# Halves for the values of the second cross attention, scores two rows ahead, and the float8 weight rounded among the experts

## What is computed

```
def _L1_xattn_ref(query, key, value, Wq, bq, Wk, bk, Wv, bv, Wo, bo):
    q = query @ Wq.T + bq;  k = key @ Wk.T + bk;  v = value @ Wv.T + bv
    attn = softmax(einsum('bqh,bkh->bqk', q, k) * 64 ** -0.5, axis=1)   # over the 100 queries
    return (attn @ v) @ Wo.T + bo

def fp8_gemm_optimized(x, input_scale, kernel, kernel_scale):
    x_q = (x / input_scale[0]).astype(float8_e4m3fn)
    k_q = (kernel / kernel_scale[0]).astype(float8_e4m3fn)
    return (x_q @ k_q) * (input_scale[0] * kernel_scale[0])
```

## Time and profile before

| | us |
|---|---|
| median of 3 runs | 1007.02 (1004.06 to 1007.10) |
| profiled execution, time | 1005.17 |
| profiled execution, span | 1003.4 |
| TensorE busy | 927.7 (92%) |
| VectorE busy | 429.6 (43%) |
| ScalarE busy | 346.2 (35%) |
| GpSimd busy | 250.9 (25%) |
| mean TensorE clock granted | 0.956 |

### The profile page before, as it was taken

The page is one execution under the profiler, slowest core; times in us unless marked ns, Lnnn a source line. Parts: engine busy times, 40 slices in busy tenths (PEclk is TensorE's granted clock), DMA queues, the critical chain, the costliest instruction groups (busy, mean ns, idle before and its releaser), DMA issues. The chain is left out here.

```text
span 1003.4 us, 19157 instructions
## 1 busy us (share of the span) xinstructions
PE 927.7 (92%) x7712; PEld 747.4 (74%) x7712; DVE 429.6 (43%) x994; ACT 346.2 (35%) x886; POOL 250.9 (25%) x306
## 2 busy tenths in 40 slices
PE   5999999989998889999999999998989899999992
PEld 5977776677775634789999999996865568999531
DVE  3973454224442656002112233136267731656576
ACT  3422332245552123122232233334266612221374
POOL 5451111023554316000000000005065403000275
PEclk9999999999999979899999999997969999999996
DMA  9993000245732707149999888801050032971001
GB/s 251 382 350 111 2 2 2 101 165 189 251 127 95 286 16 245 46 168 387 355 385 328 269 282 270 273 16 43 1 157 3 2 117 82 318 247 68 1 15 50
DMA packets 72456, 162.01 MB, mean 161 GB/s; under 512 B 4132, under 2 KB 5685, under 8 KB 70321
## 3 DMA queue, kind: packets, MB, share of 16 engines
q1 hardware_dynamic: 70048, 156.54, 45.7%
q0 software_dynamic: 2320, 4.25, 1.4%
HBM read 128.81 MB, written 31.97 MB: 160 GB/s over the span
## 5 line engine op out<-in xcount | busy, mean ns | idle before, releaser
L2108 PE MATMUL ps<-ffn_h,ffn_w 128*128 128x128 f32 x1280 | 149.1, 275 | 0.0
L2108 PEld LDWEIGHTS ps<-ffn_h,ffn_w 128*128 128x128 f32 x1280 | 145.9, 192 | 0.0
L2108 PE MATMUL ps<-ffn_xh,ffn_w 128*128 128x128 f32 x640 | 74.9, 275 | 0.3 <-ACT ffn_xh L2142 0.3
L2198 DVE TENSOR_SCALAR ffn_h<-ps,tile_bias 128x128 f32<-128x128 f32 x80 | 22.5, 345 | 122.4 <-PE ps L2108 122.4
L2108 PEld LDWEIGHTS ps<-ffn_xh,ffn_w 128*128 128x128 f32 x640 | 73.1, 192 | 0.9 <-issue 0.9
L1413 POOL TENSOR_TENSOR ctx_low<-shelf,ctx_high 128x1024 fp32r<-128x1024 f32 (+2 forms) x24 | 43.0, 1824 | 65.3 <-ACT ctx_high L1366 65.3
L2156 ACT ACTIVATE ffn_y<-ffn_y 128x128 f32<-128x128 f32 x80 | 23.7, 298 | 73.9 <-DVE ffn_y L2214 73.9
L2214 DVE SCALAR_TENSOR_TENSOR ffn_y<-ps,tile_bias,ffn_gate_row 128x128 f32<-128x128 f32 x80 | 22.6, 345 | 58.0 <-PE ps L2108 57.9
L1521 PE MATMUL ps<-x_qT,ctx_ct 128*128 128x100 f32 (+1 forms) x384 | 44.8, 278 | 2.3 <-PEq L137 2.0
L1521 PEld LDWEIGHTS ps<-x_qT,ctx_ct 128*128 128x128 f32 (+1 forms) x384 | 43.3, 191 | 3.7 <-issue 3.2
L2826 POOL TENSOR_TENSOR att_e<-att_e,decay 100x400 f32<-100x400 f32 x32 | 32.7, 1033 | 45.8 <-DVE att_e L2677 45.8
(11 more groups left out here) (467 smaller groups left out, 2086.6 us busy)
## 6 DMA issues: line engine op xcount, KB each, us to landing
ffn_w<-in_L_ffn_w_dram SPq DMA_DIRECT2D x60, 1024.0 KB, 5.9
shelf<-in_ctx_dram SPq DMA_DIRECT2D x12, 1280.0 KB
expert_rows<-nothing SPq DMA_DIRECT2D x1, 14820.0 KB, 49.7
context_turned<-ctx_ct SPq DMA_DIRECT2D x8, 1444.0 KB, 7.8
ctx_ct<-context_turned SPq DMA_DIRECT2D x8, 1444.0 KB, 13.8
ctx_lent<-in_ctx_dram SPq DMA_DIRECT2D x4, 1280.0 KB
rows_own<-expert_rows SPq DMA_DIRECT2D x8, 260.0 KB, 2.9
x_wo<-in_L_xattn_Wo_dram SPq DMA_DIRECT2D x1, 2048.0 KB, 8.9
```

The source lines that it names most:

```text
L2108: mm = nc.tensor.matmul(acc(n)[:, m, :], w[:, n % SLOTS, k, m * P:(m + 1) * P], into[l][:, i % 2, k, :], start=k == 0, stop=k == C - 1, sk ...
L2198: nc.vector.tensor_scalar(h2[:, i % 2, m, :], acc(n)[:, m, :], bsel[:, m, i, 1:2], 0.0, ALU.add, ALU.max).then_inc(h2_kept, 1)
```

## The change

Four edits, in one version.

1. context_columns: values from halves. ScalarE rounds the raw context (split, four pieces: columns 2 x 512, 2 x 512, 512, 512) and the shares (high_of_p), VectorE takes the rests (low_of_raw, low_of_p), TensorE does 18 float32r products of 512 columns per row with the shares stationary, and the result, now queries by features, is copied (keep_natural), turned by four transposes (turn_out) and copied again (keep_out). raw_low overwrites the raw row.
2. TensorE's order: scores(0), scores(1), then for each b scores(b+2), turn_out(b-1), value(b).
3. The context of this layer uses the three own buffers alone, and SP asks for turned row b+1 ahead of context row b.
4. kernel_piece goes to the expert stage: the weight and its scale are loaded at the end of the list `last`, and a piece follows every second unit from unit_at[10, 0] on. Both loads and a reciprocal leave the second self attention.

```
-        RAWS = 5
+        RAWS, OWN_RAWS = 5, 3
...
+            slot = b % (RAWS, OWN_RAWS)[layer]
...
                 @block.sync
                 def _(sp):
+                    sp.wait_ge(scored, 2)
+                    load_turned(sp, 2)
                     for b in range(2, B):
-                        if b >= RAWS:
-                            sp.wait_ge(used, b - RAWS + 1)
+                        if b + 1 < B:
+                            sp.wait_ge(scored, 2 * b)
+                            load_turned(sp, b + 1)
+                        if b >= OWN_RAWS:
+                            sp.wait_ge(used, b - OWN_RAWS + 1)
                         load_context(sp, 1, b)
-                        sp.wait_ge(scored, 2 * (b - 1))
-                        load_turned(sp, b)
...
-                    def value(b, c):
...
+                    def value(b):
+                        pe.wait_ge(low_p, b + 1)
+                        if b >= 1:
+                            pe.wait_ge(natural_a, b)
                         for j in range(KT):
+                            pe.wait_ge(low_raw, len(PIECES) * b + (j // 2 + 1 if j < KT - 1 else len(PIECES)))
+                            r = slice(0, keys(j))
+                            products = times(pp[r, b % 2, j, :], Pair(raw_high[b % 2], raw_low[b % OWN_RAWS])[r, j, :])
+                            for n, (p_, c_) in enumerate(products):
+                                mm = nc.tensor.matmul(ps[0:T, VB, :], p_, c_, start=j == 0 and n == 0,
+                                                      stop=j == KT - 1 and n == 2)
+                        mm.then_inc(used, 1)
...
+                    def turn_out(b):
+                        pe.wait_ge(natural_a, b + 1)
+                        if b >= 2:
+                            pe.wait_ge(out_kept, b - 1)
+                        for c in range(C):
+                            mm = nc.tensor.transpose(flip_bank(b)[:, c, :], an[:, b % 2, c * P:(c + 1) * P], ident[0:T, 0:T])
+                        mm.then_inc(flipped, 1)
 
                     scores(0)
+                    scores(1)
                     for b in range(B):
-                        if b + 1 < B:
-                            scores(b + 1)
-                        for c in range(C):
-                            value(b, c)
+                        if b + 2 < B:
+                            scores(b + 2)
+                        if b:
+                            turn_out(b - 1)
+                        value(b)
+                    turn_out(B - 1)
...
+                    split(0, range(4))
                     expo(0)
+                    high_of_p(0)
+                    expo(1)
                     for b in range(B):
+                        if b:
+                            keep_natural(b - 1)
                         if b + 1 < B:
-                            expo(b + 1)
-                        keep_a(b)
+                            high_of_p(b + 1)
+                            split(b + 1, range(4))
+                        if b:
+                            keep_out(b - 1)
+                        if b + 2 < B:
+                            expo(b + 2)
+                    keep_natural(B - 1)
+                    keep_out(B - 1)
...
+                    low_of_raw(0, (0, 1))
                     shift(0)
+                    low_of_raw(0, (2, 3))
                     share(0)
+                    shift(1)
+                    low_of_p(0)
                     for b in range(B):
+                        if b:
+                            count(b - 1)
                         if b + 1 < B:
-                            shift(b + 1)
                             share(b + 1)
-                        beside(dve, b)
-                        count(b)
+                            low_of_p(b + 1)
+                            low_of_raw(b + 1, range(4))
+                        if b + 2 < B:
+                            shift(b + 2)
+                    count(B - 1)
...
+        PIECE_AT = {unit_at[10, 0] + 2 * b: b for b in range(B)}
...
+                        (kernel_rows, natural(g["L1_ffn_kernel"]), in_kernel),
+                        (sc_k[:, 0:1], g["L1_ffn_kernel_scale"].partition_broadcast(P), in_kernel)]
...
+                    if n in PIECE_AT:
+                        b = PIECE_AT[n]
+                        if b == 0:
+                            dve.wait_ge(in_kernel, 32)
+                            nc.vector.reciprocal(sc_k[:, 1:2], sc_k[:, 0:1]).then_inc(k_step, 1)
+                        kernel_piece(dve, b)
...
-            sp.dma_start(kq[:].rearrange("p (c d) -> p c d", c=C), natural(g["L1_ffn_kernel"])).then_inc(in_f8[0], 16)
...
-            sp.dma_start(sc_k[:, 0:1], g["L1_ffn_kernel_scale"].partition_broadcast(P)).then_inc(in_f8[0], 16)
...
-                        nc.vector.reciprocal(sc_k[:, 1:2], sc_k[:, 0:1]).then_inc(ones, 1)
```

123 lines of the change are left out of this document (74 added, 49 removed).

## The result

The kernel after takes 1009.89 us (median of 11 runs, 1007.39 to 1011.51), the kernel before, run beside it, 1006.29 us (11 runs, 1002.33 to 1007.36): ratio 1.0033, 95% interval 1.0021 to 1.0046, so 2.1 to 4.6 us slower. The profiled execution of after took 1007.39 us, its span is 1005.6 us.

The account below looks back on a forecast made before the run. The prediction took a ring over VectorE and ScalarE, 11.0 us a row, as the bound. The next stage 3.2 us later, or 4.2 with low clock, put on a mean of 1005.8, gave 1010.0 us; range 1005 to 1015.

Parts of the forecast that it names:

- the stretch: Second cross attention, from the start of scores 1 to the next stage's first instruction; 85.0 us in the kernel before.
- The ring: Second cross attention: shares, high of shares, first high piece, low pieces, shift, exponentials follow one another each row, 11.0 us.
- my low bound: The ring's shortest row, 10.7 us, with low pieces and the shares' high half at their low bounds.
- TensorE's row: TensorE's work per row of the second cross attention: scores, values, transposes, row sums, 10.2 us against 11.15 before.
- Rival 1: TensorE remains the bound in the second cross attention, but faster: next stage 6.3 us earlier, 999.5 us; chance 0.07.
- The beginning: Start of the second cross attention: scores 2 wanted at 856.3, its turned row landing in time at 856.1.
- Rival 3: The turned row for scores 2 comes late, TensorE idles 6 us and low clock follows: 1014 us; chance 0.12.
- The wait at the end: TensorE idles 4.2 us ahead of row 5's transposes, whose copy stands behind expo(7) in ScalarE's queue.
- Half clock: After the idle at the end, values 6 ends 1.6 to 1.8 us later, of which about 0.9 shows.
- The weight: Moving the float8 weight's pieces from the second cross attention to the experts costs 0 us.
- rival 4: Low pieces slowed to 4.0 us by SBUF traffic, engine changes 0.08 each: ring 11.6, 1014 us; chance 0.08.

Follow-up runs that it names:

- Both cuts of the ring: The kernel after with VectorE's shift ahead of the low pieces (1006.11 us), and the kernel after with low pieces of rows 1 to 7 on GpSimd (1005.82 us).
- e4: The kernel before with only the float8 weight's move to the expert stage: 1006.06 us, ratio 1.0004 to before.
- e9: The kernel after with the float8 weight's pieces made beside the rows of the second cross attention, none among the experts: 1014.64 us, ratio 1.0101 to before.
- e1: The kernel after with VectorE's shift of row b+2 ahead of the low pieces of row b+1: 1006.11 us, ratio 1.0005 to before.
- e2: The kernel after with the low pieces of rows 1 to 7 made by GpSimd instead of VectorE: 1005.82 us, ratio 0.9999 to before.
- e3: The kernel after with ScalarE's copy of values 5 ahead of the exponentials of row 7: 1008.28 us, ratio 1.0036 to before.
- e12: The kernel after with scores one row ahead, as in before, and ScalarE's and VectorE's orders to match: 1013.12 us, ratio 1.0053 to before.
- e8: e7 with shift of row 1 ahead of row 0's shares, and values 6 in the scores' bank ahead of row 5's transposes: 1013.16 us, ratio 1.0079 to before.
- e7: e1 with ScalarE's exponentials of row b+2 ahead of the split of row b+1: 1013.76 us, ratio 1.0082 to before.
- e5: The kernel after with SP's turned row behind the wait for a free context buffer, as in before: 1088.07 us in a single run.
- e11: e1 with shift of row 1 ahead of row 0's shares and several steps of the last rows reordered: 1006.79 us, ratio 0.9998 to before.
- e10: e8 with a fourth context buffer and each context row asked for a row earlier: 1013.39 us, ratio 1.0085 to before.
- e13: e11 with context row 7 asked for right behind row 6, and row 7's high of shares between its split's halves: 1002.58 us, ratio 0.9969 to before.

## Why the prediction was right

Forecast 1010.0 us, slower by 4.2; measured 1009.89, slower by 3.3 (2.1 to 4.6). The mechanism was the one forecast. That the two times agree to 0.1 us is luck: the forecast starts from 1005.8 for before, whose median here is 1006.29, and its loss of 4.2 is too large by about as much against the 3.6 between the medians. Step by step, the stretch forecast was 939.6 - 850.44 = 89.2, measured 88.8:

- **The ring: right, 0.3 too long.** Forecast 11.0, measured 10.67, from hand-over to hand-over: shares 1.85 (forecast 1.86), high of shares 0.61 (0.74), first high piece 1.08 (1.04), low pieces 3.48 (3.63), shift 1.89 (2.0), exponentials 1.76 (1.72). I had added a change of engine where neighbours on one engine overlap. It is under my low bound of 10.7 by a hair. Both cuts of the ring gave 10.33: shown.
- **TensorE's row: 10.33, not 10.2.** Values 4.34 and not 4.2, 0.29 from the transposes to the values. This hit nothing in after, but it is what a cut of the ring can win: 0.8 a row, not 0.95. Rival 1 would have been 7 x 0.13 worse than priced.
- **The beginning: 0.7 too early.** I let scores 2 start at 5.9 us behind scores 1; it took 6.56, 1.17 of it a wait for a shift that stands behind the shares of row 0 on VectorE, an order that I had not added up. The turned row was no part of it: the first landing was 6.0 us as taken, and no scores waited for a transfer. Rival 3 is out. (Its idle was misread besides: with scores 1 done at about 855.6 and scores 2 at 863.9 it would have been 8.3 us and not 6.) The landings of ctx_ct after, as in the earlier trace rows:

```profile
DMA to landing us min/median/max: 6.0/11.8/13.3
```

- **The wait at the end: place and cause right,** 3.52 against 4.2, smaller as the ring is.
- **Half clock: undersized.** I counted 0.9 of 1.7 us as showing. Values 6 ended at about 930.0, where full speed would have given 922.70 + 0.36 + 4.34 = 927.4, so 2.6 us more; ScalarE was free at 928.1 and the copy started at 930.19, so 2.1 us showed. Six turns of the ring at 0.32 less (1.9) made up for this (1.2 more than counted) and for the beginning (0.7): the errors cancel, which is luck again, and the 0.4 by which the stretch is shorter than forecast is spread over the copies and transposes of the end.
- **The weight: 0,** shown by e4. But its value lies in the pair (e9), which I hadn't priced: I wrote that it doesn't help the second stage, meaning the kernel before.
- **Low pieces slowed (rival 4):** 1.22 and 0.68 us, as in the earlier trace rows. Out.

The rule cited in the prediction (the Trainium skill, "TensorE: Matmul & The Clock Gate", section "What's actually happening": the throttled state is the default, activity lifts it) agrees with the trace of after: 0.50 granted behind the 3.52 us of idle. It doesn't tell which idle brings the low clock; see the last section.

Over all kernels the stretch accounts for the time: against before -0.6, 0.0, 3.2, 3.8, 7.1, 8.2, 9.2, 10.0 and 81.6 us of stretch (e1, e2, e3, after, e12, e8, e7, e9, e5) go with 0.5, -0.1, 3.6, 3.3, 5.3, 7.9, 8.2, 10.2 and 81.8 us of time (the ratio's excess times 1006; for e5 the difference of the times), within about 2 us. So do 0.0, 0.2, 8.0 and -2.9 us of stretch (e4, e11, e10, e13) with 0.4, -0.2, 8.6 and -3.1.

## What to carry to other kernels

When three engines pass a tile around, write down each engine's order and add up every closed ring, not the busy time of each engine: here 10.67 us a row came from engines busy 18.8 and 13.4 of 25 us. Do it again for each reordering, since a second swap can join two rings that ran beside each other (e7). When a stage gets shorter, look next at the transfers' landing and at the last rows, where nothing lies beside the chain; and price a pair of edits as a pair. When a number comes out as forecast, look whether the event that was to bring it did happen: in e13 the row asked for earlier didn't land earlier.

## What the runs showed of the hardware that was not expected

**Two transfer engines bring up the rear.** In e11_tail_in_order context row 7 was asked for at 910.80 and landed at 925.29. Windows (last two columns: DMA share, GB/s):

```profile
914.00:916.00 2.00, 2.00 (x21) 2.00 (x21) 1.23 (x3) 0.70 (x1) 0.00 (x0) 1.00 1.06 305
...
918.00:920.00 2.00, 2.00 (x10) 1.41 (x9) 0.44 (x1) 1.53 (x2) 0.00 (x0) 1.00 0.13 49
920.00:922.00 2.00, 2.00 (x19) 1.23 (x18) 2.00 (x3) 2.00 (x5) 0.00 (x0) 1.00 0.13 47
```

By 918 the stream had thinned out; from there a share of 0.13, two of 16 engines, moved 49 and 47 GB/s up to 922, and less up to the landing. The context row's last piece is 82 partitions (L792). The Trainium skill, "DMA: Bandwidth & Descriptors", section "Why a DMA increments its semaphore by 16 and not by 1", says that a copy is spread over the largest number of engines up to 16 that divides the slowest dimension of both sides; for 82 that is 2, and the trace agrees. An estimate from the sizes in the profile's list of DMA issues and the share of two engines: per row those two carry 2/16 of 1444 and of 1280 KB and all of 164 KB, 504 KB, which at 49 GB/s is 10.5 us. The splits of e1_shift_ahead that waited for context rows came 11.3 and 11.1 us apart. Context row 7 has no turned row ahead of it: 2/16 of 1280 KB and 164 KB are 324 KB, 6.8 us by the same estimate, and its split started 6.82 us behind that of row 6 in e11 and 6.75 in e13, although it was asked for 10.3 us behind row 6 in the one and 2.8 in the other. So the row's rate of transfer seems to be set by the 82-partition piece; this is argued from two matches and was not tried. Cutting it into 80 and 2 partitions would be the next thing to measure.

**GpSimd slows VectorE's two-tensor instructions.** In e2 the share product took 1.23 us on average instead of 0.78 and the low shares, which read two tensors too, 0.88 instead of 0.78, and the one-tensor sum stayed at 0.78. The Trainium skill, "SBUF — State Buffer", section "SBUF: two separate sides", offers a reason: VectorE and GpSimd share a port pair under an exclusive lock, which a VectorE instruction with two SBUF inputs takes against a GpSimd one that reads SBUF. The trace agrees in which instructions suffer.

**An issue can hold SP for long.** An issue that takes 0.38 us elsewhere took 7.32 in e13 (L791 at 896.49), while a turned row and a context row asked for before it were still under way; the one behind it (L793 at 903.85) took 3.09. Asking earlier in the program is then not asking earlier in time.

**The opening's clock varies by itself.** Scores 0 took 6.99 us in the profile of before and 8.62 in that of e4, whose stage is the same code; in after it was the longer kind, granted 0.50 from 840 to 846, against 844 to 846 in before. Up to 1.6 us of an execution's time is this, which a comparison of two profiles must leave out.

**The length of an idle doesn't tell the clock behind it.** The same place of the stage, values 6 behind the wait for the transposes of row 5, as windows of e1_shift_ahead (2.05 us of idle) and of e2_low_on_pool (2.59 us):

```profile
924.00:925.00 1.00, 1.00 (x4) 0.62 (x3) 0.71 (x1) 1.00 (x2) 0.00 (x0) 0.50 0.00 0
922.00:923.00 1.00, 1.00 (x6) 0.73 (x5) 1.00 (x1) 0.00 (x0) 1.00 (x2) 1.00 0.00 0
```

The shorter idle was followed by 0.50 and the longer by 1.00. In e9_weight_beside waits of 1.71 and 1.46 us ahead of scores 4 and 6 were followed by scores of 7.02 us instead of 5.39, in e13_last_row_early one of 1.42 by full clock. What decides between them stays open.
